# Scores in three PSUM banks, first-pass chunks in two, and GpSimd masking two rows of probabilities at once

## The chip, the core and the metric

The kernel runs on one NeuronCore of a Trainium2 chip, as one program launched once. The metric is the device time in microseconds; three runs are timed, and their median counts. TensorE multiplies into PSUM (eight banks of 128 x 512 float32), VectorE and ScalarE read PSUM, GpSimd works on SBUF alone, and SP issues most of the DMAs.

## The reference

The input is x of shape (8, 1024, 128). Two blocks follow one another, each with a residual sum:

```
x = x + attention(layernorm(x))      # 8 heads of 16, relative positions, softmax over 1024 keys, output projection
x = x + moe(layernorm(x))            # router, best 2 of 8 experts, each (128 -> 2 x 512, gelu gate, 512 -> 128)

xh      = layernorm(inputs)*gamma+beta, split into heads
q, k, v = xh @ Wq + bq, xh @ Wk + bk, xh @ Wv + bv
p       = positions @ Wp
score   = ((q + u) . k + rel_shift((q + v) . p)) / sqrt(128)
ctx     = softmax(score) . v
```

`rel_shift` makes the position score of query q and key k come from position k - q + 1023 for k <= q, zero for k = q + 1, and from the next query's row above that. The kernel handles this with two forms of the operands, one for the lower triangle (QL) and one for the upper (QU), against a common K.

## The kernel before, in words

**Stages.** A prologue normalizes and projects the first batches and runs the first pass of two heads. A hardware loop over the 8 batches follows, with the engines' programs written out for 8 heads of 9 units each (`h`, `u`). Behind it a short tail finishes the last batch and the router's tables, and the expert stage (`expert_phase`) works through the routed tiles. The change touches the first two stages and renames a few banks of the tail.

**Two passes over the scores.** Softmax needs the row maximum first, so each head's scores are computed twice. The first pass (`first_pass`, lines 654 to 676) runs two heads ahead (`AHEAD = 2`): 18 chunks a head, 16 of them of 128 queries by 512 keys and two (positions 8 and 12 of `ORDER`) of four 128x128 diagonal blocks. TensorE writes chunk n to the PSUM bank `pA[n % S1_BUFS]`; VectorE reads it with a masked sum and maximum (lines 1084 and 1090) and counts `s1_read`. TensorE waits for that count before it overwrites the bank: `S1_BUFS` is 3. After a head's chunks VectorE reduces the maxima (`mneg`, 1098) and subtracts them from the super-diagonal score (`dsup`, 1100). The negated maxima go through TensorE, an evacuation and a DMA (`maximum_row`) into one row of the operands.

The second pass (`second_pass`, 678 to 697) has for each head one unit of the 8 upper diagonal blocks (u = 0) and one for each block row of keys (u = 1 to 8), each in two halves of 512 queries. Halves 0 and 1 of every unit use the two halves of `pB` (two banks). ScalarE's exponentials (986, 988) write them to `upper_diag` or to the ring `prob` of four rows. A half is overwritten when its own exponential of the unit before is done (`p_exp`).

**The order on TensorE.** In each unit: score half 0, chunk 2u, score half 1, chunk 2u + 1; then in the units of `PAIRS_AT` = 1, 4, 6, 8 the contexts of two block rows (`context`, line 708, four column strips each); then the small matmuls that `M_AT`, `W_AT`, `PROJECT_AT` and `UPPER_AT` place at this (h, u): maximum rows, turned contexts, output projection, router, and the projections of later batches. Those go to the banks `pM` and `pE`. With pC for the contexts all eight banks are taken: 3 + 2 + 1 + 1 + 1.

**The order on the others.** VectorE: chunk 2u, a small evacuation if `DVE_OUT` has one here, chunk 2u + 1, then other work placed by (h, u): the normalizing of the contexts (1118 to 1128), statistics, the router, and `low` (1069), which subtracts the rounded high half of an operand from the operand (halves of c, k, gl, gu, eight in a batch; gu is read from PSUM). ScalarE: the two exponentials, then evacuations. GpSimd: after a unit's exponentials it masks (`affine_select`) the upper diagonals (564), or, for a block row, sets one element (569), masks its 128x128 diagonal block (571) and adds the upper one (576); then work placed by (h, u): positions (480 to 492), reciprocal roots, residual bias, and the row scatters (518). `context` waits for `p_mask`, the exponential of a later row for `pv_done`. SP loads a head's operands (`stack`), and stores the split operands (`store`) of the next batch in heads 2, 3 and 4, on `hi_done` and `low_done`.

The lines as the profile numbers them:

## Time and profile before

| | us |
|---|---|
| median of three runs | 1681.2 (1679.35 to 1681.27) |
| the profiled execution | 1680.72 |
| its span, first to last instruction | 1679.0 |
| TensorE busy | 1548.0 (92%) |
| VectorE busy | 1397.8 (83%) |
| ScalarE busy | 1108.9 (66%) |
| GpSimd busy | 1103.0 (66%) |
| mean share of the full TensorE clock granted | 0.952 |

An engine's busy time is the union of its instructions' times. TensorE's ends are modelled, since matmuls are pipelined, so a busy TensorE may still be waiting; PEld is its weight loading, which runs beneath the matmul before, and whose start is where a wait ends. The loop lasts from about 87 to 1236 us. Inside it the chain of what ended last can't be read from the page, because the page's chain covers the expert stage; the stretches, waits and timeline below are used for it.

### The profile page before, as it was taken

Reading aid. Unit: us, or ns where it says so; the run is one execution under the profiler, and the core shown is the slowest. Engines: PE = TensorE matmul, PEld = TensorE weight load, DVE = VectorE, ACT = ScalarE, POOL = GpSimd, SP = SyncE. Lnnn points to the kernel's source line nnn. Section 1 sums busy time; section 2 is a strip of 40 time slices with the busy share of each in tenths; the row PEclk is TensorE's granted clock in tenths of the full one; section 3 lists DMA queues with packets and bytes.
Section 4 is the critical chain, followed back from the end, with each engine's and each line's share of the span. In section 5 each row is a group of like instructions: output and inputs, shape, how many; then the busy total and the mean of one; then the engine's idle time right before and its main releaser. Section 6 shows DMA issues by size and latency. Waiting matters only on the chain. (4 is left out here: it accounts for less than half of the span.)

```text
span 1679.0 us, 50905 instructions
## 1 busy us (share of the span) xinstructions
PE 1548.0 (92%) x12492; PEld 1204.6 (72%) x12493; DVE 1397.8 (83%) x5262; ACT 1108.9 (66%) x2295; POOL 1103.0 (66%) x2088
## 2 busy tenths in 40 slices
PE   3789999999999999999999999999952699999997
PEld 1567776677777767777777776776741699999997
DVE  4669899989989987998998899899864588887886
ACT  2157777776777776677777777767730477777775
POOL 5247767767766775777677677667673276666665
PEclk8679999999999998999999999999985799999999
DMA  5746535535644553464365355346454244444443
GB/s 136 198 116 174 148 93 152 164 96 128 180 116 128 161 148 84 110 203 110 104 174 148 93 141 164 97 129 179 122 153 136 42 58 54 56 56 52 56 53 49
DMA packets 133844, 199.72 MB, mean 119 GB/s; under 512 B 20888, under 2 KB 95016, under 8 KB 133632
## 3 DMA queue, kind: packets, MB, share of 16 engines
q1 hardware_dynamic: 108064, 177.07, 39.0%
q0 software_dynamic: 25568, 20.14, 8.2%
q8 instruction: 94, 1.54, 0.4%
q14 instruction: 118, 0.97, 0.2%
HBM read 108.10 MB, written 75.20 MB: 109 GB/s over the span
## 5 line engine op out<-in xcount | busy, mean ns | idle before, releaser
L1084 DVE CUSTOM_DVE_ANT_0 junk<-pA,lmask 128x512 bf16<-128x512 f32 x1056 | 686.9, 683 | 65.1 <-PE pA L671 45.9
L986 ACT ACTIVATE prob<-pB 128x512 f32<-128x512 f32 x384 | 229.8, 598 | 205.5 <-PE pB L690 115.9
L1578 POOL DMA_INDIRECT out<-yb,dst x142 | 230.4, 1622 | 131.3 <-ACT yb L1656 78.5
L692 PE MATMUL pB<-QL,K 97*128 97x512 f32 (+3 forms) x768 | 286.4, 373 | 1.4 <-ACT upper_diag L986 1.2
L669 PE MATMUL pA<-K,QL 96*128 96x512 f32 (+3 forms) x792 | 282.1, 357 | 5.1 <-DMA K<-split_operands 3.4
L690 PE MATMUL pB<-QU,K 97*128 97x512 f32 (+3 forms) x640 | 267.5, 418 | 0.2
L671 PE MATMUL pA<-K,QU 96*128 96x512 f32 (+3 forms) x660 | 233.1, 354 | 4.4 <-DVE acc L1084 3.2
L988 ACT ACTIVATE prob<-pB 128x512 f32<-128x512 f32 x384 | 227.9, 594 | 12.7 <-PE pB L692 3.4
L708 PE MATMUL pC<-prob,vext 128*17 128x256 f32 x3088 | 217.8, 385 | 0.1
L576 POOL TENSOR_TENSOR prob<-prob,upper_diag 128x128 f32<-128x128 f32 x384 | 179.7, 468 | 31.9
L690 PEld LDWEIGHTS pB<-QU,K 97*128 97x128 f32 x640 | 122.0, 191 | 99.9 <-issue 62.3
L518 POOL DMA_INDIRECT routed_rows<-sent,sent_to x144 | 156.9, 1089 | 29.7 <-issue 24.3
L569 POOL MEMSET prob<- 1x1 f32 x384 | 33.9, 88 | 205.6 <-ACT prob L988 197.9
L669 PEld LDWEIGHTS pA<-K,QL 96*128 96x128 f32 x792 | 153.5, 194 | 14.0 <-DVE acc L1084 4.5
L1090 DVE CUSTOM_DVE_ANT_0 junk<-pA,umask 128x128 bf16<-128x128 f32 x528 | 122.2, 284 | 44.1 <-PE pA L675 41.3
L692 PEld LDWEIGHTS pB<-QL,K 97*128 97x128 f32 x768 | 147.3, 192 | 15.7 <-ACT upper_diag L986 2.8
L671 PEld LDWEIGHTS pA<-K,QU 96*128 96x128 f32 x660 | 128.1, 194 | 22.2 <-DVE acc L1084 14.5
L1699 DVE SCALAR_TENSOR_TENSOR g<-pLin,b_all,gl 128x256 f32<-128x256 f32 x288 | 125.8, 478 | 21.4 <-issue 7.9
L708 PEld LDWEIGHTS pC<-prob,vext 128*17 128x17 f32 x3088 | 78.2, 98 | 84.3 <-issue 22.8
L1607 PE MATMUL pY<-w_all,g 128*128 x1136 | 138.4, 275 | 0.0
L1607 PEld LDWEIGHTS pY<-w_all,g 128*128 128x128 f32 x1136 | 133.1, 192 | 0.0
L1649 ACT ACTIVATE gl<-pGate,b_all 128x256 f32<-128x256 f32 x288 | 119.2, 464 | 12.1 <-PE pGate L1601 8.4
(305 smaller groups left out, 3642.9 us busy)
## 6 DMA issues: line engine op xcount, KB each, us to landing
QL<-split_operands SPq DMA_DIRECT2D x67, 256.0 KB
QU<-split_operands SPq DMA_DIRECT2D x67, 256.0 KB
K<-split_operands SPq DMA_DIRECT2D x67, 256.0 KB
xg<-routed_rows SPq DMA_DIRECT2D x75, 132.0 KB
split_operands<-c_h SPq DMA_DIRECT2D x36, 256.0 KB, 6.1
split_operands<-c_l SPq DMA_DIRECT2D x36, 256.0 KB, 6.4
QL<-split_operands SPq DMA_DIRECT2D x67, 128.0 KB
QU<-split_operands SPq DMA_DIRECT2D x67, 128.0 KB
```

The lines of the kernel that those rows point to most:

```text
L518: po.indirect_dma_start(dram["xs"], bass.IndirectOffsetOnAxis(sent_to[:, t, j:j + 1], 0), sent[:, t, :], None).then_inc(scattered, 16)
L576: po.tensor_tensor(p, p, upper_diag[h % 2][:, P * kb:P * kb + P], ALU.add).then_inc(p_mask, 1)
L669: mm = pe.matmul(dst[:, 0:low], QL[0:KROWS, s, q], K[0:KROWS, s, k0:k0 + low], start=True, stop=True)
L671: mm = pe.matmul(dst[:, low:HALF], QU[0:KROWS, s, q], K[0:KROWS, s, k0 + low:k0 + HALF], start=True, stop=True)
L690: mm = pe.matmul(pB[:, q0:q0 + up], K[0:r, s, k], QU[0:r, s, q0:q0 + up], start=True, stop=True)
L692: mm = pe.matmul(pB[:, q0 + up:q0 + HALF], K[0:r, s, k], QL[0:r, s, q0 + up:q0 + HALF], start=True, stop=True)
L708: mm = pe.matmul(pC[VW * strip:VW * strip + D + 1, :], vext[:, kb, h % H, :], prob[kb % RING][:, quarter * strip:quarter * strip + quarter ...
L986: act.activation(p[:, 0:HALF], pB[:, 0:HALF], ACT.Exp, scale=SCALE).then_inc(p_exp, 1)
L988: act.activation(p[:, HALF:S], pB[:, HALF:S], ACT.Exp, scale=SCALE).then_inc(p_exp, 1)
L1084: v.tensor_tensor_reduce(out, src[:, :], lmask[:, at:at + HALF], 1.0, -3.0e38, ALU.add, ALU.max, acc[:, s, qb, n % 2:n % 2 + 1]).then_inc( ...
L1578: po.indirect_dma_start(dram["out"], bass.IndirectOffsetOnAxis(dst[k][:, a:a + 1], 0), yb[k][:, a, :], None, compute_op=ALU.add).then_inc( ...
L1607: mm = pe.matmul(pY[k % 2][:, a, :], g[k % 2][:, c, P * a:P * a + P], keep["w2"][:, bass.ds(ex * F + c * E, E)], start=(c == 0), stop=(c = ...
```

## The change

- PSUM: `S1_BUFS` goes from 3 to 2. `pB` becomes three single banks, and the halves of all units, in order, go round them (`S2_BUFS = 3`, counter g = 2 (9 h + u) + half). A score half waits for the exponential three halves back instead of two.
- TensorE's order: in units with contexts the next unit's score half 0 is issued before the two contexts, not after them and the small matmuls.
- GpSimd masks block rows in pairs, in the even units: two memsets, one select and one addition over both diagonal blocks. For this the ring's rows lie two by two in one tensor (`keep["b2"]` is twice as wide).
- Six of the eight `low` halves of a batch (c, k, gl) and the eight `dsup` differences go from VectorE to GpSimd, the former at `SPLIT_AT`, the latter in unit 3 (`DSUP_AT`). The two halves of gu stay on VectorE and get a semaphore of their own, `gu_low`.
- Places of GpSimd's other work move by a unit or two (positions, residual, scatters). In prologue and tail, `pB[2]` takes the place of the third pA bank.

```diff
-S1_BUFS = 3
+S1_BUFS = 2
+S2_BUFS = 3
...
-        prob = [keep["b2"]] + [sb(f"prob{i}", [P, S]) for i in range(1, RING)]
+        ring = [keep["b2"], sb("prob23", [P, 2, S])]
+        prob = [ring[i // 2][:, i % 2, :] for i in range(RING)]
...
-        pB, pC = pb("pB", [P, S]), pb("pC", [P, S // STRIPS])
+        pB, pC = [pb(f"pB{i}", [P, HALF]) for i in range(S2_BUFS)], pb("pC", [P, S // STRIPS])
...
-        LOW_AT = {(1, 2): 0, (2, 3): 1, (2, 7): 2, (3, 2): 3, (3, 6): 4, (4, 1): 5, (4, 3): 6, (4, 4): 7}
-        POSITIONS_AT = ((1, 1), (1, 4), (1, 8), (2, 1), (2, 4), (2, 6), (5, 4), (5, 6))
+        LOW_AT = {(3, 6): 4, (4, 4): 7}
+        SPLIT_AT = {(0, 3): 0, (1, 8): 1, (2, 8): 2, (3, 3): 3, (3, 7): 5, (4, 2): 6}
+        DSUP_AT = 3
+        POSITIONS_AT = ((1, 1), (1, 3), (1, 7), (2, 1), (2, 3), (2, 5), (5, 5), (5, 7))
...
-        SCATTER_AT = ((0, 1), (0, 4), (0, 6), (0, 8), (1, 6), (3, 1), (3, 6), (3, 8), (4, 4), (4, 6), (5, 1), (5, 8), (6, 1), (6, 4), (6, 6), (6, 8))
+        SCATTER_AT = ((0, 1), (0, 5), (0, 7), (0, 8), (1, 5), (3, 1), (3, 5), (4, 5), (4, 7), (5, 1), (5, 3), (6, 1), (6, 3), (6, 5), (6, 7), (7, 5))
...
+            def low(nb, n):
+                name, half = SPLITS[n]
+                cut = slice(HALF * half, HALF * half + HALF)
+                src = {"c": qu, "k": kc, "gl": g_lo}[name][:, cut]
+                have = known(po, nb * HI_N + n + 1)
+                po.wait_ge(set_pool, POOL_SET)
+                po.wait_ge(hi_done, have)
+                po.tensor_tensor(parts[name][1][:, cut], src, parts[name][0][:, cut].bitcast(F32), ALU.subtract).then_inc(low_done, 1)
+            def super_difference(b, h):
+                ...
+                po.wait_ge(mx_done, have)
+                po.tensor_tensor(dsup[:, s, :], acc[:, s, :, 3], mneg[:, s, :].bitcast(F32), ALU.add).then_inc(dsup_done, 1)
...
-                        else:
-                            kb = u - 1
-                            if kb > 0:
-                                po.memset(prob[kb % RING][0:1, P * kb - 1:P * kb], 0.0)
-                            p = prob[kb % RING][:, P * kb:P * kb + P]
+                        elif u % 2 == 0:
+                            kb = u - 2
+                            both_rows = ring[kb // 2 % 2][:, :, :].rearrange("p a s -> p (a s)")
+                            for k in (kb, kb + 1)[kb == 0:]:
+                                po.memset(prob[k % RING][0:1, P * k - 1:P * k], 0.0)
+                            p = both_rows.rearrange("p (n q) -> p n q", q=P)[:, kb:kb + NB + 2:NB + 1, :]
                             po.affine_select(out=p, in_=p, compare_op=ALU.is_ge, fill=0.0, base=0,
-                                             pattern=[[1, P]], channel_multiplier=-1).then_inc(lower_masked, 1)
+                                             pattern=[[0, 2], [1, P]], channel_multiplier=-1).then_inc(lower_masked, 1)
...
-                            po.tensor_tensor(p, p, upper_diag[h % 2][:, P * kb:P * kb + P], ALU.add).then_inc(p_mask, 1)
+                            po.tensor_tensor(p, p, upper_diag[h % 2][:, P * kb:P * kb + 2 * P].rearrange("p (n q) -> p n q", q=P), ALU.add).then_inc(p_mask, 2)
+                        if u == DSUP_AT:
+                            super_difference(b, h + 1)
+                        if (h, u) in SPLIT_AT:
+                            low(b + 1, SPLIT_AT[h, u])
...
-                pe.wait_ge(p_exp, HPB * (b * (H * S2U) + h * S2U + u) + half + 1)
-                r, q0 = MROW + 1, HALF * half
+                g = HPB * (h * S2U + u) + half
+                pe.wait_ge(p_exp, HPB * (b * (H * S2U)) + max(g, 1))
+                r, q0, dst = MROW + 1, HALF * half, pB[g % S2_BUFS]
...
-                        second_pass(b, h, u, 0)
+                        if (h, u) == (0, 0) or (u - 1) % S2U not in PAIRS_AT:
+                            second_pass(b, h, u, 0)
                         first_pass(b, h + AHEAD, 2 * u)
                         second_pass(b, h, u, 1)
                         first_pass(b, h + AHEAD, 2 * u + 1)
                         if u in PAIRS_AT:
+                            if (h, u) != (H - 1, S2U - 1):
+                                second_pass(b, h + (u + 1) // S2U, (u + 1) % S2U, 0)
                             back, kb = PAIRS_AT[u]
                             context(b, h + back, kb)
                             context(b, h + back, kb + 1)
...
+                                    pe.wait_ge(low_done, (b + 1) * LOW_N + LOW_N)
...
-                v.wait_ge(mx_done, b * H + h + 1)
-                v.tensor_tensor(dsup[:, s, :], acc[:, s, :, 3], mneg[:, s, :].bitcast(F32), ALU.add).then_inc(dsup_done, 1)
...
                 elif name == "super":
+                    v.wait_ge(dsup_done, b * H + H)
                     super_out(src, done)
```

## Rows read from the trace of the kernel before

**Rows 1.** Stretches of the kernel: us, then busy time (instructions) of each engine, clock, DMA share.

```profile
0.00:87.00 87.00, 45.79 (x139) 28.17 (x140) 48.44 (x174) 18.05 (x29) 33.30 (x61) 0.75 0.61 161
...
87.00:1236.00 1149.00, 1133.98 (x9272) 811.29 (x9272) 1033.44 (x4233) 831.39 (x1680) 803.34 (x1848) 0.99 0.49 135
...
1313.00:1679.00 366.00, 352.53 (x3010) 351.94 (x3010) 287.24 (x721) 254.41 (x577) 230.38 (x142) 0.98 0.40 53
```

**Rows 2.** The same view for two batches of the loop.

```profile
237.28:378.78 141.50, 139.93 (x1159) 100.35 (x1159) 129.06 (x529) 103.84 (x211) 100.55 (x231) 1.00 0.50 136
...
520.29:668.07 147.78, 146.29 (x1159) 104.37 (x1159) 129.39 (x529) 104.07 (x211) 100.55 (x231) 0.95 0.47 131
```

**Rows 3.** Waits in 237.28 to 378.78: total us, times, longest.

```profile
PEld pB L696 <- ACT prob L988: 3.0, 7, 0.4
...
PEld pB L690 <- ACT b_all L988: 1.7, 4, 0.4
...
PEld pB L690 <- ACT prob L986: 1.5, 4, 0.5
...
PEld pA L671 <- DVE acc L1084: 1.1, 3, 0.5
...
PEld pM L761 <- DVE hr L1183: 1.3, 1, 1.3
```

**Rows 4.** Groups in that batch, count | busy, mean ns | idle before.

```profile
L708 PE MATMUL pC<-prob,vext 128*17 128x256 f32 x384 | 26.8, 381 | 0.0
...
L708 PE MATMUL pC<-b_all,vext 128*17 128x256 f32 x128 | 10.0, 385 | 0.0
...
L1100 DVE TENSOR_TENSOR dsup<-acc,mneg 128x8 f32<-128x8 f32 x8 | 2.1, 265 | 0.3
...
L1069 DVE TENSOR_TENSOR k_l<-kc,k_h 128x512 fp32r<-128x512 f32 x2 | 1.4, 680 | 0.0
```

**Rows 5.** Timeline, third head of a batch: start, us, engine, line [idle <-releaser].

```profile
708.26 0.67 DVE L1084 CUSTOM_DVE_ANT_0 junk<-pA,lmask 128x512 bf16<-128x512 f32 x1
...
708.83 0.60 ACT L986 ACTIVATE prob<-pB 128x512 f32<-128x512 f32 x1 [0.34 <-PE pB L692]
...
709.00 0.19 PEld L671 LDWEIGHTS pA<-K,QU 96*128 96x128 f32 x1 [0.25 <-DVE acc L1084]
...
709.48 0.19 PEld L690 LDWEIGHTS pB<-QU,K 97*128 97x128 f32 x1 [0.23 <-ACT prob L986]
...
709.77 0.52 PEld L675 LDWEIGHTS pA<-K,QU 96*128 96x128 f32 x4
...
710.07 0.62 ACT L986 ACTIVATE prob<-pB 128x512 f32<-128x512 f32 x1
...
712.01 0.19 PEld L669 LDWEIGHTS pA<-K,QL 96*128 96x128 f32 x1
```

**Rows 6.** Timeline, a load of pA and its read, twice.

```profile
777.52 0.19 PEld L669 LDWEIGHTS pA<-K,QL 96*128 96x128 f32 x1
...
778.25 0.69 DVE L1084 CUSTOM_DVE_ANT_0 junk<-pA,lmask 128x512 bf16<-128x512 f32 x1 [0.33 <-PE pA L671]
...
779.51 0.19 PEld L669 LDWEIGHTS pA<-K,QL 96*128 96x128 f32 x1
...
780.17 0.69 DVE L1084 CUSTOM_DVE_ANT_0 junk<-pA,lmask 128x512 bf16<-128x512 f32 x1 [0.61 <-PE pA L669]
```

**Rows 7.** Timeline, VectorE and GpSimd side by side.

```profile
671.34 1.22 DVE L1118 TENSOR_TENSOR vsh<-vsh,psup 128x1024 f32<-128x1024 f32 x1
...
671.52 1.35 POOL L576 TENSOR_TENSOR b_all<-b_all,upper_diag 128x128 f32<-128x128 f32 x1 [0.17 <-POOL b_all L571]
```

**Rows 8.** GpSimd's groups in 237.28 to 378.78.

```profile
L576 POOL TENSOR_TENSOR prob<-prob,upper_diag 128x128 f32<-128x128 f32 x48 | 22.3, 465 | 4.0
...
L571 POOL TENSOR_SCALAR_AFFINE_SELECT prob<-prob 128x128 f32<-128x128 f32 x48 | 15.0, 312 | 0.0
...
L483 POOL TENSOR_TENSOR g_lo<-rp,cos_lo 128x512 f32<-128x512 f32 x2 | 2.6, 1280 | 0.0
```

More of the change, by code:

```diff
@@ L161, in attention_phase @@
         e_ready, e_done, hi_done = sem("e_ready"), sem("e_done"), sem("hi_done")
-        ln, low_done, pos, norm, rs_done, res_done = (sem(n) for n in ("ln", "low_done", "positions", "norm", "rs_done", "residual_biased"))
+        ln, low_done, gu_low, pos, norm, rs_done, res_done = (sem(n) for n in ("ln", "low_done", "upper_low", "positions", "norm", "rs_done", "residual_biased"))
         placed, moved = sem("head_values_placed"), sem("values_shifted")
@@ L292, in store @@
             def store(nb, name):
-                highs, lows = known(sp, nb * HI_N + READY[name]), known(sp, nb * LOW_N + READY[name])
+                highs, lows = known(sp, nb * HI_N + READY[name]), known(sp, nb * GU_N + GU_N if name == "gu" else nb * LOW_N + LOWS[name])
                 sp.wait_ge(set_dve, DVE_SET)
                 sp.wait_ge(hi_done, highs)
-                sp.wait_ge(low_done, lows)
+                sp.wait_ge(gu_low if name == "gu" else low_done, lows)
                 for op, row in PLACES[name]:
@@ L316, in _ @@
                 sp.wait_ge(hi_done, READY[name])
-                sp.wait_ge(low_done, READY[name])
+                if name == "gu":
+                    sp.wait_ge(gu_low, GU_N)
+                else:
+                    sp.wait_ge(low_done, LOWS[name])
                 store_side(name, 0)
@@ L609, in project @@
                 first = nb == 0 if isinstance(nb, int) else False
-                dst = (pE, *pA)[j % 4] if first else pE
+                dst = (pE, *outside)[j % 4] if first else pE
                 if j == 0:
@@ L695, in second_pass @@
                         k = slice(k0, k0 + P)
-                        mm = pe.matmul(pB[:, k], K[0:r, s, k], QU[0:r, s, k], start=True, stop=True)
+                        mm = pe.matmul(dst[:, k0 - q0:k0 - q0 + P], K[0:r, s, k], QU[0:r, s, k], start=True, stop=True)
                 mm.then_inc(s2_ready, 1)
@@ L788, in small_piece @@
                 elif part == 0 and name == "values 0":
-                    pe.wait_ge(low_done, (b + 1) * LOW_N + LOW_N)
+                    pe.wait_ge(gu_low, (b + 1) * GU_N + GU_N)
                 elif part == 0:
@@ L870, in _ @@
             pe.wait_ge(m_done, m_at(B, "rows 1") + 1)
-            router_hidden(range(NB), pA[1]).then_inc(m_ready, 1)
-            router_fold(B, pA[2]).then_inc(m_ready, 1)
-            router_logits(B, pB[:, 0:HALF]).then_inc(m_ready, 1)
-            router_ranks(B, pB[:, HALF:S]).then_inc(m_ready, 1)
+            router_hidden(range(NB), outside[1]).then_inc(m_ready, 1)
+            router_fold(B, outside[2]).then_inc(m_ready, 1)
+            router_logits(B, pB[0]).then_inc(m_ready, 1)
+            router_ranks(B, pB[1]).then_inc(m_ready, 1)
         @block.scalar
@@ L887, in evacuate @@
                 half = slice(HALF * (j % 2), HALF * (j % 2) + HALF)
-                src = (pE, *pA)[j % 4] if isinstance(nb, int) and nb == 0 else pE
+                src = (pE, *outside)[j % 4] if isinstance(nb, int) and nb == 0 else pE
                 if j < 2:
@@ L1037, in _ @@
                 copied(f"rows {j}", (pE, pA[0])[j], m_done)
-            fold(B, pA[2])
+            fold(B, outside[2])
             tanh(B)
@@ L1068, in low @@
                 v.wait_ge(hi_done, nb * HI_N + n + 1)
-                v.tensor_tensor(parts[name][1][:, cut], src, parts[name][0][:, cut].bitcast(F32), ALU.subtract).then_inc(low_done, 1)
+                v.tensor_tensor(parts[name][1][:, cut], src, parts[name][0][:, cut].bitcast(F32), ALU.subtract).then_inc(gu_low if name == "gu" else low_done, 1)
             def super_out(src, done):
@@ L1299, in _ @@
                 stats(1, t)
-            for n in range(4, LOW_N):
+            for n in range(4, HI_N):
                 low(0, n)
@@ L1370, in _ @@
                 v.wait_ge(w_ready, B * W_N + 1 + j)
-                final(j, pA[1 + j], w_done)
+                final(j, outside[1 + j], w_done)
                 router_stats(B, range(4 * j, 4 * j + 4))
@@ L1375, in _ @@
             v.wait_ge(m_ready, m_at(B, "hidden") + 1)
-            router_bias(B, pA[1])
+            router_bias(B, outside[1])
             hidden_stats(B)
@@ L1386, in _ @@
             v.wait_ge(m_ready, m_at(B, "ranks") + 1)
-            places(B, 0, pB[:, HALF:S])
+            places(B, 0, pB[1])
             for part in (1, 2):
```

37 lines of the change are left out of this document (22 added, 15 removed).

## Prediction

> **What bounds the kernel now.** I read the stretches first: of the 1679.0 us, the loop over the eight batches takes 87 to 1236 us, with TensorE busy for 1134 of 1149, VectorE 1033, ScalarE 831, GpSimd 803; the expert stage after it (366 us, TensorE 352.5 busy) is not touched [rows 1]. So the time is eight times one batch, and a batch at full clock is 141.5 us; one with the clock at 0.95 is 147.8 with the same instructions [rows 2]. Two engines are near that length, TensorE (139.9 busy) and VectorE (129.1). Matmul ends are modelled, so I work out TensorE's own time from starts. Four pieces of 128 columns follow one another by 0.11 (the group at 709.77, of which the last load is 0.19: 0.52). From there to the load at 712.01 are 2.24 us with no other piece: the four (0.44), three runs of 512 columns at 2.4 GHz with their switch, 0.23 each, and so 1.11 for a pair of contexts [rows 5]. A head has 16 score halves and 16 chunks of 0.23, two of each in four pieces (0.45), and four pairs of contexts: 4.58 + 4.58 + 4.44 = 13.6, or 108.6 a batch. The remaining matmuls are 1159 less 384 + 128 of contexts, and by the loops 240 of scores and 240 of the first pass: 167 [rows 2, 4]; at the 0.11 of a 128-column piece, and less for the ranks', 17.5. Own time 126.1, waits 15.4.
>
> Who ends the waits, in the table of waits of one batch: ScalarE's exps 3.0 + 1.7 + 1.5 = 6.2, VectorE's reads of pA 1.1, a VectorE result (the router's hidden rows) 1.3 [rows 3]. The other 6.8 lie under modelled ends; shared out alike, scores cost 11.1, first-pass banks 2.0, results 2.3.
>
> **The score side (removed).** Before, each half of pB is written again only after its exp: the exp of 708.83 ends at 709.43, the load follows at 709.48 and its exp starts at 710.07 [rows 5]: 0.05 + 0.59 + 0.60 = 1.24 a unit, while TensorE alone needs 0.92. With three banks a half waits for the exp three halves back: three per 1.24 is more than TensorE can issue, so the waits on exps go: -11.1 a batch. Issuing the next unit's first half ahead of the contexts adds no matmul; its maximum row was sent four units earlier. ScalarE gets work beneath the contexts except where pv_done still holds it (units 5 and 7: one context, 0.5). ScalarE's 103.8 [rows 2] does not bind.
>
> **The first pass (added).** Chunk k now waits for VectorE's read of k-2. The cycle: the read at 708.26 takes 0.67, and the load waiting for it starts at 709.00, 0.07 after its end [rows 5]; a load at 779.51 has its read start at 780.17 into an idle VectorE, 0.66, and in two pieces, 777.52 to 778.25, 0.73 [rows 6]. Cycle 0.69 + 0.07 + 0.66 = 1.42 per two chunks, against 0.92 of TensorE and 1.22 (2 x 0.61) of VectorE back to back. Three banks made that 1.42 for three chunks, which never bound. I write out a head from loads of chunks, all else absent. Units 0 and 1: chunk 2 waits to 1.48 (TensorE is there at 1.14), chunk 3 to 2.10 (1.94), chunk 4 at 3.67. Units 2 and 3: chunk 6 to 1.48 (0.92), 7 to 2.09 (1.94), 8 to 2.90 (2.55). Units 5 and 7: 0.56 each and 0.15 in the latter. The waits are 0.34, 0.16, 0.56, 0.15, 0.35, 0.56, 0.56 and 0.15: 2.83 a head, 22.6 a batch. But nearly all of the 167 small matmuls stand in units without contexts, after the second chunk and before the waiting one. Set place by place against the waits (for each head and unit the lesser of both) they fill 13.0: 1.7 in unit 0, 2.0 in 2, 2.0 in 3, 4.1 in 5, 3.2 in 7. Left: 9.6. Bounds: 2.0 (the waits of before, if PE work covers the rest) and 22.6.
>
> **VectorE's other work.** Six low halves go to GpSimd (0.68 each) and eight differences of 0.27 [rows 4]: 4.1 + 2.1 = 6.2. The two upper halves stay. So VectorE falls to 122.9. Its chunks are 8 x (16 x 0.61 + 2 x 0.86) = 91.8, leaving 31 of other work. With two banks VectorE is empty during each pair of contexts: from my head, 0.96 after unit 1, 0.68 after 4, 0.66 after 6, 1.23 after 8, 28.2 a batch. The pieces placed there by the code fit but for 2.6 (such as 1.22 in one lump [rows 7]); about 7.8 stand in units without contexts, where they lengthen the cycle directly; formerly a third chunk in store hid them. I take 0.7 of 2.6 and half of 7.8, since the small matmuls stand at the same places: 5.7; bounds 0 and 10.4.
>
> Sum of a batch after: 126.1 + 9.6 + 2.3 + 5.7 = 143.7, 2.2 more than now, 17.6 for eight.
>
> **GpSimd.** A pair of rows now takes two memsets (0.09, overlapping), a select of 256 columns and an addition of 256. The select of 128 is 0.31, so of 256 between that and 0.62; I take 0.42, as its fixed part is large. From 128 and 512 columns (0.465 and 1.280) the addition is 0.74 [rows 8]; with their hand-over 1.3, against 2 x 0.87 before. 32 pairs save some 12 a batch; six low halves of 1.28 and eight differences of 0.2 add 9.3. It stays near 98 of 143. The first row of a pair is ready a unit later than before, but contexts of a pair come two units after its exps: the mask is done about 2.9 us into unit 2 and wanted at 4.0. I cost it at nothing; without that cover it is 0.3 to 0.5 a pair. Low halves arrive before the stores that take them (heads 2, 3, 4), and the last, which gates head 5's reload, is the unmoved upper one. Waits added: super_out on dsup_done (met three units earlier; DVE chunks are behind it), project 0 on low_done (met two heads earlier), the mask's own (as before). SP's queue keeps its order.
>
> **Ends.** The 36 first-pass chunks ahead of the loop have only VectorE at 0.61 and a TensorE at 0.75 of its clock in that stretch [rows 1]. The cycle there is at least 1.42 against 1.22 for half the chunks, but projects between them hide some: +2 (0 to 6). In the tail other banks are named; the waits it moves are met.
>
> Total 1680.7 (the profiled run; 1.7 outside its span) + 17.6 + 2 = 1700. The three timed runs have the median 1681.2, within 0.5 of it.
>
> **GpSimd's port.** A masking addition of 128x128 took 1.35 us at 671.52, beneath a VectorE product of 1.22 that reads two SBUF tensors, against 0.465 as a rule [rows 7, 8]. The Trainium skill, GPSIMD Engine Reference, section Specifications, says that GpSimd shares its SBUF interfaces with VectorE where the latter has two SBUF inputs; the trace agrees. By that rule the pair's mask is held as one, contexts and then TensorE wait, and the sum would be rival 4's, where without it the masks cost nothing.
>
> **Rivals.**
> 1. The score side decides, faster. The first-pass cycle fills wholly with small matmuls and VectorE's lumps fall in its holes: waits on pA fall to about 4, lumps to 1. 126.1 + 4 + 2.3 + 1 = 133.4 is the end; halfway between that and 143.7 is 138.5, or -24, with the +2 of the start 1659. For it: VectorE loses 6.2 us, and the waits on exps that the table names are six times those on pA [rows 3]. Against it: the cycle 1.42 is longer than 1.24. It holds if waits on pA plus lumps stay under 13.1 a batch.
> 2. The two first-pass banks bind, much slower. The mechanism is the 1.42 cycle in units without contexts with only half of the 13.0 filled: 143.7 + 6.5 = 150.2, +70 and +2: 1752. Against it: small matmuls are there in the trace. It is slower from 13.1 on.
> 3. Both cancel, no change: within 0.2% (3.4 us, what a measurement of this kernel can tell from none): 1681. The engines trade one cycle for the other.
> 4. Masks in pairs come late: about seven stretches of VectorE in a batch read two SBUF tensors for as long as that 1.22 (the sums over vsh, the router's normalizing); each holds an addition by 1.35 - 0.465 = 0.9, and if half of that reaches TensorE it is 3.2 a batch on top of 143.7, so 1726. Against it: the pair's mask has a unit to spare, as worked out above.
>
> **Chances.** Forecast 0.40 (its own range 1685 to 1720, from 7 to 12 left over of the first-pass waits and 4 to 8 of lumps), rival 1 0.34, rival 2 0.12, rival 3 0.10, rival 4 0.04. Part of the forecast's lower edge meets rival 3. Faster 0.35, same 0.10, slower 0.55. The range reaches from 1648 (two thirds of rival 1) to 1738 (the lower half of rival 2); a dip of the clock as in the fourth batch, 6.3 us [rows 2], is within it either way.
>
> **What would show it.** Right: TensorE's waits on ScalarE near zero; loads of pA waiting for VectorE in most units 2, 3, 5, 7, first-pass loads 1.4 apart from the chunk two before; VectorE busy 123 a batch with longer idle stretches after contexts; a batch of 143 to 145. The masking addition 0.74, select 0.42, low halves 1.28 on GpSimd. Wrong: a batch under 141, pA loads hardly waiting (then the small matmuls fill more than place by place), or contexts waiting for GpSimd's addition.

## The result, and the profile after

The changed kernel takes 1732.6 us (median of four runs, 1728.2 to 1736.2), the kernel before 1681.2 (four runs, 1679.4 to 1690.4): a ratio of 1.0293, 95% interval 1.0249 to 1.0337. It is slower by 51, where 19 were forecast (17.6 in the batches and 2 at the start). The profiled execution's span is 1730.9 against 1679.0.

The stretches of the kernel after, in the view of [rows 1]: start, loop, expert stage.

```profile
0.00:97.00 97.00, 53.70 (x144) 32.66 (x146) 49.01 (x172) 18.06 (x29) 33.54 (x62) 0.67 0.56 147
97.00:1288.00 1191.00, 1161.69 (x9253) 817.69 (x9252) 1009.37 (x4121) 835.00 (x1679) 771.85 (x1448) 0.98 0.47 130
1365.00:1731.00 366.00, 352.00 (x3010) 351.42 (x3010) 287.34 (x721) 254.36 (x577) 232.55 (x143) 0.98 0.40 53
```

Two batches of it, one with a dip of the clock (to be laid beside [rows 2]):

```profile
400.10:552.55 152.45, 149.12 (x1159) 105.08 (x1159) 126.44 (x515) 104.42 (x211) 96.55 (x182) 0.96 0.46 126
698.95:845.26 146.31, 143.01 (x1159) 101.10 (x1159) 126.11 (x515) 104.30 (x211) 96.57 (x182) 1.00 0.48 132
```

A batch at full clock went from 141.5 to 146.3 with the same 1159 matmuls. The 52 us fall into: the start, whose first exp of the loop moved from 88.2 to 97.1 (+8.8); eight batches of +4.85 (+38.8); the clock, which beyond the loop's first 13 us stood at its lower level for 31 us of the loop after and for 17 before, a little under half of which is lost, and what else the first batch differs by (+5); and the rest (-0.6). The expert stage is the same.

Where the time went, in the table of waits of the second of these batches (total, times, longest), against [rows 3]:

```profile
PEld pA L702 <- DVE acc L1123: 10.4, 25, 1.1
...
PEld pC L742 <- issue: 6.6, 25, 0.4
...
PEld pA L702 <- issue: 5.9, 13, 0.7
...
PEld pA L704 <- DVE acc L1123: 3.9, 11, 0.6
...
PEld pM L796 <- DVE hr L1220: 1.1, 1, 1.1
```

All waits on ScalarE are gone from it, and VectorE's reads took their place: 14.3 us listed in two rows where 1.1 stood in one. But a part of either list is no wait of that kind. The first load behind each of the 32 pairs of contexts in a batch finds TensorE's loading idle for 0.42 us, before and after, whoever is named as its releaser. Before, that is 18 loads of pB named "issue" (7.6 us, no releaser), 12 named an exp (5.1) and 2 of pM; after, 18 named a read of VectorE (7.6). Without these, waits on exps were 1.9 us in 5 places before, and waits on VectorE's reads went from 1.4 to 8.0.

The masks' groups in the same batch, against [rows 8]:

```profile
L605 POOL TENSOR_TENSOR prob<-prob,upper_diag 128x256 f32<-128x256 f32 x17 | 14.1, 831 | 2.5
L605 POOL TENSOR_TENSOR b_all<-b_all,upper_diag 128x256 f32<-128x256 f32 x16 | 12.2, 760 | 2.4 <-POOL b_all L600 0.2
...
L600 POOL TENSOR_SCALAR_AFFINE_SELECT prob<-prob 128x256 f32<-128x256 f32 x16 | 6.5, 404 | 0.0
...
L511 POOL TENSOR_TENSOR c_l<-qu,c_h 128x512 fp32r<-128x512 f32 x2 | 2.6, 1281 | 0.0
...
L519 POOL TENSOR_TENSOR dsup<-acc,mneg 128x8 f32<-128x8 f32 x8 | 1.6, 206 | 2.2 <-ACT prob L1027 2.1
```

Select 0.40, addition 0.76 to 0.83, low half 1.28, difference 0.21, where the prediction had 0.42, 0.74, 1.28 and 0.2.

The start, in the timeline after at the lower clock: reads of chunks come in twos.

```profile
77.10 0.69 DVE L1123 CUSTOM_DVE_ANT_0 junk<-pA,lmask 128x512 bf16<-128x512 f32 x1
77.24 0.29 PEld L702 LDWEIGHTS pA<-K,QL 96*128 96x128 f32 x1 [0.97 <-DVE acc L1123]
...
78.18 0.69 DVE L1123 CUSTOM_DVE_ANT_0 junk<-pA,lmask 128x512 bf16<-128x512 f32 x1 [0.39 <-PE pA L704]
...
78.80 0.69 DVE L1123 CUSTOM_DVE_ANT_0 junk<-pA,lmask 128x512 bf16<-128x512 f32 x1
```

The load at 77.24 had its bank back 0.14 into the read that started at 77.10, and its own read starts at 78.18, 0.94 later (0.73 at full clock for such a chunk in two pieces [rows 6]). So two chunks take 78.80 - 77.10 = 1.70 at the lower clock, not 1.42; before, with three banks, reads came 0.61 apart at the lower clock too, 1.22 for two.

### The profile page after: what moved, and what is told of

It is laid out like the page before. It is cut to its first block and busy times, and to the rows that moved or that the text cites. A ratio compares the mean times of both kernels' runs of the same rounds, so it can differ in the third digit from the quotient of the medians.

```text
span 1730.9 us, 50465 instructions
## 1 busy us (share of the span) xinstructions
PE 1583.4 (91%) x12492; PEld 1214.9 (70%) x12493; DVE 1374.3 (79%) x5148; ACT 1112.8 (64%) x2295; POOL 1074.6 (62%) x1689
## 5 line engine op out<-in xcount | busy, mean ns | idle before, releaser
L1123 DVE CUSTOM_DVE_ANT_0 junk<-pA,lmask 128x512 bf16<-128x512 f32 x1056 | 696.7, 686 | 113.3 <-PE pA L704 81.9
L702 PE MATMUL pA<-K,QL 96*128 96x512 f32 (+3 forms) x792 | 321.4, 407 | 25.9 <-DVE acc L1123 13.4
L724 PE MATMUL pB<-QU,K 97*128 97x512 f32 (+3 forms) x640 | 246.0, 384 | 0.0
L704 PE MATMUL pA<-K,QU 96*128 96x512 f32 (+3 forms) x660 | 242.3, 369 | 3.4 <-DVE acc L1123 2.4
L1025 ACT ACTIVATE prob<-pB 128x512 f32<-128x512 f32 x256 | 153.2, 598 | 94.8 <-PE pB L726 41.6
L1025 ACT ACTIVATE b_all<-pB 128x512 f32<-128x512 f32 x256 | 152.5, 596 | 86.0 <-PE pB L724 46.2
L1027 ACT ACTIVATE b_all<-pB 128x512 f32<-128x512 f32 x256 | 152.8, 597 | 80.4 <-PE pB L726 71.7
L1027 ACT ACTIVATE prob<-pB 128x512 f32<-128x512 f32 x256 | 152.6, 596 | 45.8 <-PE pB L726 37.7
L742 PE MATMUL pC<-b_all,vext 128*17 128x256 f32 x2048 | 139.5, 391 | 0.0
L742 PE MATMUL pC<-prob,vext 128*17 128x256 f32 x2064 | 138.2, 386 | 0.8 <-POOL prob L605 0.8
```

The source lines that it names most:

```text
L702: mm = pe.matmul(dst[:, 0:low], QL[0:KROWS, s, q], K[0:KROWS, s, k0:k0 + low], start=True, stop=True)
L704: mm = pe.matmul(dst[:, low:HALF], QU[0:KROWS, s, q], K[0:KROWS, s, k0 + low:k0 + HALF], start=True, stop=True)
L724: mm = pe.matmul(dst[:, 0:up], K[0:r, s, k], QU[0:r, s, q0:q0 + up], start=True, stop=True)
L742: mm = pe.matmul(pC[VW * strip:VW * strip + D + 1, :], vext[:, kb, h % H, :], prob[kb % RING][:, quarter * strip:quarter * strip + quarter ...
L1025: act.activation(p[:, 0:HALF], pB[HPB * n % S2_BUFS][:, :], ACT.Exp, scale=SCALE).then_inc(p_exp, 1)
L1027: act.activation(p[:, HALF:S], pB[(HPB * n + 1) % S2_BUFS][:, :], ACT.Exp, scale=SCALE).then_inc(p_exp, 1)
```

## The experiments

All batches below are at full clock, first exp to first exp. Ratios are by the timed runs, with the 95% interval, to the kernel before as it was timed again beside each group of runs (1682.6 to 1684.9, so only the changed kernel's ratio is over 1681.2). In e10 part of the probabilities keeps old values, so its results aren't the layer's.

| run | banks: chunks, scores | batch | loop begins | median | ratio |
|---|---|---|---|---|---|
| before | 3, 2 | 141.5 | 88.2 | 1681.2 | |
| after | 2, 3 | 146.3 | 97.1 | 1732.6 | 1.0293 (1.0249 to 1.0337) |
| e1 banks only | 2, 3 | 146.2 | 98.1 | 1732.5 | 1.0281 (1.0255 to 1.0307) |
| e2 moves only | 3, 2 | 143.1 | 89.3 | 1694.5 | 1.0059 (1.0042 to 1.0075) |
| e3 two and two | 2, 2 | 146.3 | 96.4 | 1725.1 | 1.0249 (1.0204 to 1.0293) |
| e4 start on three | 2, 3 | 146.3 | 88.8 | 1720.4 | 1.0217 (1.0188 to 1.0245) |
| e5 five in common | 5 | 141.8 | 91.1 | 1685.2 | 1.0011 (0.9986 to 1.0037) |
| e6 the same, with the moves | 5 | 142.0 | 91.1 | 1691.7 | 1.0048 (1.0025 to 1.0071) |
| e7 after, order of before | 2, 3 | 146.6 | 97.3 | 1727.1 | 1.0253 (1.0193 to 1.0312) |
| e8 after, half reads | 2, 3 | 139.7 | 94.1 | 1668.6 | 0.9912 (0.9876 to 0.9949) |
| e9 before, half reads | 3, 2 | 138.7 | 84.3 | 1659.9 | 0.9845 (0.9793 to 0.9898) |
| e10 neither bound | 5 | 137.6 | 84.7 | 1657.5 | 0.9831 (0.9788 to 0.9874) |
| e12 pairs only | 3, 2 | 142.4 | 91.4 | 1693.4 | 1.0048 (1.0018 to 1.0077) |
| e13 before, half chunks | 3, 2 | 128.9 | 85.4 | 1592.2 | 0.9444 (0.9390 to 0.9498) |
| e14 after, half chunks | 2, 3 | 129.4 | 90.2 | 1591.2 | 0.9438 (0.9360 to 0.9515) |
| e15 low halves and places | 3, 2 | 142.7 | 91.0 | 1696.8 | 1.0067 (1.0040 to 1.0094) |

The medians hold their share of the clock's dips (e1 and e3 have the same batch and differ by 7 in the median), so conclusions are drawn from batches.

**Which part costs.** e1 has the change's edits of banks and order alone, e2 the other edits alone, e3 takes the bank from the chunks and gives it to nobody in the loop (`S1_BUFS = 2`, `S2_BUFS = 2`, the order of before).

```diff
 e1 on before:                            e2 on after:
-S1_BUFS = 3                             -S1_BUFS = 2
+S1_BUFS = 2                             -S2_BUFS = 3
+S2_BUFS = 3                             +S1_BUFS = 3
+(first half ahead of the contexts)      +S2_BUFS = 2
                                         -(first half ahead of the contexts)
```

> The kernel before with the bank change alone (two first-pass banks, three score banks, the next unit's first half ahead of the contexts); VectorE keeps its low halves, differences and the places of its small work, GpSimd masks row by row. Theory A, the two first-pass banks bring the whole loss of the loop (4.85 us a batch, 146.35 against 141.5), and VectorE's 6.2 us a batch of moved work only softened it: a batch of 147.5 to 149.5, 1742 to 1758. Rival B, the banks are neutral and the loss comes from what went to GpSimd and from the new places of the small work: a batch near 142, 1690 to 1700 with the slower start.

> The changed kernel with three first-pass banks and two for the scores again, and the order of the matmuls of before; pairs of rows, low halves and differences on GpSimd stay. Theory A: the loss is gone, and since VectorE was not what the chain of before waited for in most units, its 6.2 us a batch bring little: a batch of 140 to 141.5, 1668 to 1682. Rival B: masks in pairs and low halves from GpSimd are late: a batch of 144 to 146, 1700 to 1718.

> The kernel before with two first-pass banks and two score banks (one bank for nothing but the start's projections), same order, nothing moved: what the lost bank costs by itself. Theory A: TensorE's waits on VectorE come on top of those on ScalarE, which stay, with some of both in the same places: a batch of 150 to 157, 1760 to 1815. Rival C, the third score bank (and the half issued ahead of the contexts) does the harm and not the lost one: a batch of 142 to 144, 1690 to 1705.

One full-clock batch of e1, e2 and e3 in turn (length; TensorE, its loads, VectorE, ScalarE and GpSimd busy):

```profile
995.26:1141.46 146.20, 143.33 (x1159) 100.77 (x1159) 130.17 (x529) 104.28 (x211) 101.89 (x231) 1.00 0.47 132
```

```profile
527.99:671.08 143.09, 140.24 (x1159) 100.26 (x1159) 125.30 (x515) 103.84 (x211) 96.26 (x182) 1.00 0.49 135
```

```profile
696.38:842.68 146.30, 143.85 (x1159) 100.70 (x1159) 130.07 (x529) 104.67 (x212) 101.99 (x231) 1.00 0.46 132
```

The lost bank is the whole loss of the batches, theory A, but less than I expected of e1 and e3. e3 and e1 have the same batch to 0.1 us: the third score bank, together with the half issued ahead of the contexts, is worth nothing in sum. Their heads are not the same. The second takes 16.7 us in e1 and 17.9 in e3, the third 18.6 and 18.1, the eighth 18.7 and 18.1, from first exp to first exp. The changed kernel against e7 below, which differ in the order alone, shows the same pattern (16.2 and 17.4, 17.9 and 17.4, 18.6 and 18.0), so it is the order that moves time from head to head.

e1 and the changed kernel have the same batch too, though VectorE is busy for 130.2 in one and 126.1 in the other: with two banks its moved work is worth nothing in sum either. There too gains and losses cancel: the second and third heads are 0.6 and 0.7 shorter in the changed kernel, the first, fourth, fifth and sixth 0.3, 0.6, 0.4 and 0.3 longer. With three banks the moves cost 1.6, and e2's 143.1 lies between both theories.

**The start.** In e4 the 36 chunks ahead of the loop go round pA0, pA1 and the third score bank, each waiting for the read three chunks back.

```diff
-                dst = pA[n % S1_BUFS]
+                ahead = isinstance(b, int) and h < AHEAD
+                dst = outside[(S1U * h + n + 2) % 3] if ahead else pA[n % S1_BUFS]
```

> The changed kernel, but the 36 chunks ahead of the loop go round three banks (the third score bank is free there). The chunks' reads came 0.62 and 1.08 apart there, 1.70 for two, where they were 1.22 before, over some 18 pairs: 8.6 us, and the loop began at 97.1 instead of 88.2. Theory A': the start is the cycle over two banks at half clock, so it comes back whole: the loop begins at 88 to 89, 1724. Rival: the start lost its stretch of full clock for another reason, and the cycle is only 3.6 of it: the loop begins at 93 to 94, 1729.

Reads of that start, in e4's timeline, go from bank to bank 0.61 apart (here at full clock, in the kernel before at the lower one as well):

```profile
73.63 0.69 DVE L1129 CUSTOM_DVE_ANT_0 junk<-pA,lmask 128x512 bf16<-128x512 f32 x1
...
74.25 0.69 DVE L1129 CUSTOM_DVE_ANT_0 junk<-pB,lmask 128x512 bf16<-128x512 f32 x1
...
74.86 0.69 DVE L1129 CUSTOM_DVE_ANT_0 junk<-pA,lmask 128x512 bf16<-128x512 f32 x1
```

The loop begins at 88.8, as theory A' has it, but the two banks are not the whole of the start's loss. In this stretch the executions also differ in how long TensorE had its full clock: 10 us in the kernel before, none in the changed one, 7 us in e4. From the first read to the first exp of the loop, in before, e12, after, e3 and e4 in turn:

```profile
58.40:88.24 29.84, 24.04 (x85) 15.06 (x83) 24.68 (x102) 4.09 (x7) 2.49 (x2) 0.67 0.71 192
```

```profile
58.26:91.35 33.09, 28.96 (x85) 18.62 (x83) 24.68 (x102) 4.09 (x6) 2.49 (x2) 0.50 0.63 174
```

```profile
57.35:97.07 39.72, 30.89 (x85) 18.80 (x84) 25.25 (x100) 4.08 (x7) 2.69 (x3) 0.50 0.54 146
```

```profile
58.38:96.38 38.00, 28.91 (x85) 17.27 (x84) 25.85 (x102) 4.09 (x7) 2.49 (x2) 0.59 0.53 147
```

```profile
57.50:88.78 31.28, 26.52 (x85) 16.72 (x83) 24.31 (x100) 4.09 (x6) 2.70 (x3) 0.61 0.67 184
```

At the lower clock throughout, two banks take 39.7 (after) and three 33.1 (e12; 32.7 in e15); with 7 us at full clock 38.0 (e3) and 31.3 (e4). So the banks cost 6.6 to 7.0. The remainder of the 8.8 is the full clock that the kernel before had (33.1 - 29.8 = 3.3), less 1.1 by which the first read came earlier in the changed kernel. The missing stretch doesn't go with the banks: e12 and e15 have three and none of it, e3 and e11 have two and 7 and 14 us of it.

**Order, and banks in common.** e7 puts the score half behind the contexts again; in e5 and e6 halves and chunks, in the order in which TensorE issues them, take the next of five banks, and each waits for the reader of that bank.

```diff
 e5 and e6:
-                dst = pA[n % S1_BUFS]
+                dst = pA[bank_of(f)]
...
-                r, q0, dst = MROW + 1, HALF * half, pB[g % S2_BUFS]
+                wait_user(b, 2 * g)
+                r, q0, dst = MROW + 1, HALF * half, pA[TURN[2 * g]]
```

> The changed kernel with each score half issued where it was before, behind the contexts. Theory A: the first-pass cycle sets the batch, the half's place is worth nothing: 146.2 to 146.8 a batch, 1728 to 1738. Rival: the half ahead of the contexts holds TensorE there for its exp or gives ScalarE work, so the batch moves by over 1 us either way.

> The kernel before, but score halves and first-pass chunks, which TensorE issues in turn, take the next of five banks in common; order and everything else as before. A chunk's bank is then wanted again by the score half three further on, a half's bank by the chunk two further on: each has 2.5 of its own kind to spare, where it is 3 and 2 before. Theory A (each side has a cycle of 1.42 and 1.24 us and stops TensorE when it gets under two of a kind; at two banks the first pass alone sets the batch, 146.3 with either two or three score banks): at 2.5 both cycles are shorter than the engines' own rates, 0.57 and 0.50 us against 0.61 and 0.60, so the batch falls below 141.5, to 134 to 139: 1625 to 1665. Rival: with any bank less than three for the chunks VectorE's other work in one lump reaches TensorE, and each kind now also waits for the other engine: 143 to 146, 1695 to 1720.

> The same five common banks with the pairs of rows, low halves and differences on GpSimd. Those moves cost 1.6 us a batch with the banks of before (143.1 against 141.5) and nothing with two (146.35 against 146.25). Theory A: with five in common VectorE is nearest to the bound, and its 6.2 us less a batch are worth 1 to 3: 132 to 137. Rival D, GpSimd's later results cost wherever the banks do not: 1 to 2 a batch more than with five banks alone.

A batch of e7, e5 and e6 in turn:

```profile
549.48:696.11 146.63, 143.35 (x1159) 100.89 (x1159) 126.25 (x515) 104.92 (x210) 96.43 (x182) 1.00 0.48 131
```

```profile
239.53:381.37 141.84, 139.62 (x1159) 100.58 (x1159) 129.45 (x529) 104.19 (x212) 100.14 (x231) 1.00 0.49 136
```

```profile
239.66:381.66 142.00, 138.58 (x1159) 100.19 (x1159) 125.13 (x515) 103.83 (x210) 96.05 (x182) 1.00 0.49 136
```

The order is worth 0.3. e5 was a miss for both theories: 2.5 banks for each side ought to have freed both, and the batch is that of before. So was e6: with five banks the moves cost 0.2, neither a gain nor 1 to 2. That raised the question of whether there was anything to free.

**What is under the waits.** e8 and e9 shorten VectorE's read of the chunks off the diagonal, e10 shortens reads and most exps on five common banks, e13 and e14 shorten reads and matmuls of those chunks.

```diff
 e8, e9, e10, e13, e14:
-                    v.tensor_tensor_reduce(out, src[:, :], lmask[:, at:at + HALF], 1.0, ...
+                    v.tensor_tensor_reduce(out[:, 0:HALF // 2], src[:, 0:HALF // 2], lmask[:, at:at + HALF // 2], 1.0, ...
...
 e13, e14 besides:
+                    wide, low = HALF // 2, min(low, HALF // 2)
...
-                    if low < HALF:
-                        mm = pe.matmul(dst[:, low:HALF], ...
+                    if low < wide:
+                        mm = pe.matmul(dst[:, low:wide], ...
```

> The changed kernel, but each chunk that isn't on the diagonal is read over its first 256 columns only (the maximum then covers half of the keys; it only keeps the exps small). A read then takes some 0.4 us instead of 0.67 and the cycle some 1.15 instead of 1.42; VectorE has 128 x 0.27 = 34 us a batch less. Theory A: the two banks' cycle is what the batch waits for, so most of the waits on VectorE go (33.7 us gross of lost load time before first-pass loads): 130 to 136 a batch, 1615 to 1655. Rival: the waits are TensorE's own small matmuls and contexts, wrongly read: over 142.

> The kernel before (three first-pass banks, two score banks) with chunks off the diagonal read over 256 columns only, as in the same edit of the changed kernel, which went from 146.35 to 139.7 us a batch. Theory F (the floor is near: TensorE's own work is 137 or more a batch, not 126.1, so no cycle of banks has more than a few us to give): 138.5 to 140.5 a batch, 1650 to 1665. My prediction's numbers (own work 126.1, 11.1 of waits on the exps, 2.0 on pA): the waits on the exps stay, only 2 go: 139.5 to 141. Rival V (VectorE's 129 us of work is what sets the batch of before, TensorE has 15 to spare): under 136.

> Five banks in common, chunks off the diagonal read over 256 columns, and six of the nine rows of probabilities of a head computed over half of their columns only (the other half keeps old values, so later results are not the layer's): both cycles are gone, what is left is TensorE's own work and its waits on small results. Theory F: 136 to 139 a batch, that is, my own time of 126.1 was 8 to 11 too small and the waits of before only some 4. My prediction's own time: 126.1 + 2.3 of results: 128 to 131 a batch.

> The kernel before with chunks off the diagonal computed and read over 256 columns only (the maximum covers half of the keys). Against the same with 512 computed and 256 read (138.7 a batch) it only takes TensorE work: 14 chunks a head less 0.11 and 2 less 0.05, 13.1 us a batch. Theory F (TensorE's own work is what the batch of before is made of): most of it comes off, less what the exps' cycle of 1.24 us a unit then holds in units without contexts (0.92 - 0.22 = 0.70 of TensorE there): 128 to 134 a batch, 1580 to 1625. Rival G (another chain, GpSimd's masks or a DMA, holds the batch near 138 whatever TensorE has to do): 136.5 to 138.7.

> The same edit of the changed kernel (139.7 with half the reads alone). Theory F: TensorE's 13.1 come off here too, less what two first-pass banks hold (the cycle with short reads, some 1.15 for two chunks, against 0.70 of TensorE), while three score banks let go of the exps' cycle: 129 to 136, near the other. If it ends under that of before by over 1 us, three score banks are worth something once TensorE is out of the way. Rival G: 137.5 to 139.7.

A batch of e8, e9, e10, e13 and e14 in turn:

```profile
939.15:1078.81 139.66, 138.17 (x1159) 100.95 (x1159) 96.72 (x515) 103.25 (x211) 95.48 (x182) 1.00 0.50 138
```

```profile
519.24:657.92 138.68, 138.39 (x1159) 100.33 (x1159) 100.17 (x529) 103.93 (x212) 101.76 (x231) 1.00 0.51 139
```

```profile
657.63:795.21 137.58, 136.84 (x1159) 100.47 (x1159) 101.42 (x529) 87.25 (x211) 101.03 (x231) 1.00 0.50 140
```

```profile
628.90:757.82 128.92, 127.64 (x1128) 91.21 (x1126) 98.94 (x529) 103.78 (x212) 100.45 (x231) 1.00 0.53 150
```

```profile
614.87:744.25 129.38, 125.77 (x1128) 91.80 (x1127) 95.46 (x515) 102.24 (x212) 95.24 (x182) 1.00 0.53 149
```

The groups of reads and exps in that batch of e10:

```profile
L1114 DVE CUSTOM_DVE_ANT_0 junk<-pA,lmask 128x256 bf16<-128x256 f32 x128 | 53.3, 421 | 23.1 <-PE pA L689 13.5 <-PE pA L687 6.8
```

```profile
L1017 ACT ACTIVATE prob<-pA 128x256 f32<-128x256 f32 x48 | 18.5, 385 | 5.5 <-PE pA L721 4.8
L1015 ACT ACTIVATE prob<-pA 128x256 f32<-128x256 f32 x48 | 18.4, 384 | 30.3 <-PE pA L719 18.0 <-PE pA L721 12.3
```

With VectorE's reads (0.42 instead of 0.68) and most exps (0.38 instead of 0.60) shortened, the batch is 137.6, and TensorE's busy column, 136.8, agrees with it. The batch of before, 141.5, gave up 3.9 in all: 2.8 to the shorter reads (e9), 1.1 to the shorter exps (e10, which also changes the banks). In this batch of e10 no load waits for a read or an exp, save the 32 idle times of 0.42 us behind contexts, so some 4 us is also the most that any arrangement of banks could have given. The batch after gave up 6.6 to the reads (e8), a miss for both theories there (under 136, over 142).

Most of the 137.6 is TensorE's own work, and not another chain, by e13: taking 13.1 us of its columns away and nothing else shortens the batch from 138.7 to 128.9, by 9.8, with the same work on GpSimd and ScalarE. Loads of scores that don't stand behind contexts then wait for exps for 6.2 us, against 2.0 in e9, which may be where the other 3.3 went. Even there, where TensorE has time for ScalarE, three score banks and two first-pass banks (e14) end 0.5 behind.

**Small matmuls.** e11 and e16 issue every matmul of the loop's projections twice.

```diff
-                    mm = pe.matmul(dst[:, lo:hi], w[:, :], src[:, at + lo:at + hi], start=True, stop=True)
+                    for _ in range(1 if first else 2):
+                        mm = pe.matmul(dst[:, lo:hi], w[:, :], src[:, at + lo:at + hi], start=True, stop=True)
```

> The changed kernel with each matmul of the projections in the loop issued twice (24 of 256 columns and 8 transposes of 128 a batch): the same results, and the small work that I let fill TensorE's waits is larger by 24 x 0.22 + 8 x 0.11 = 6.2 us (the loads behind one of 256 columns are 0.22 apart, so these were undersized by half in my sum too). My prediction's rule (small matmuls fill the waits place by place): under 2 of it shows, 146.4 to 148.3. Theory F: most waits stand elsewhere and little is filled: 4.5 to 6.2 show, 150.9 to 152.5.

> The kernel before with each matmul of the projections in the loop issued twice, as in the same edit of the changed kernel: its batches, clear of dips of the clock, went up by 8 or more there, 4.8 of it in the eighth head with a stop of up to 4.2 us ahead of the next head's first scores, 1.25 in the third. Own work added: 6.2. Theory F: it is on the path here as well, 5 to 6.2 and no less in the third head than with two banks (1.25), 146.5 to 148 or more where the stop appears too. My prediction's rule (waits take it up): under 2.

Both whole times (1805.3 and 1771.7) are of little use, and both lie above what either rule had without the stop that follows. In either kernel TensorE stopped for 3.6 to 5.0 us at the end of every batch, at the load of the diagonal scores that begin the next one, and the clock dipped in every batch. The third and fourth heads are clear of both. The third has eight of the doubled matmuls, the fourth none. From first read to first read, the third head and then the fourth, in the kernel before and in e16:

```profile
415.13:431.37 16.24, 16.24 (x134) 11.39 (x133) 15.87 (x71) 11.82 (x25) 12.23 (x27) 1.00 0.67 185
431.37:449.62 18.25, 17.76 (x144) 12.35 (x142) 16.93 (x63) 13.76 (x28) 13.83 (x35) 1.00 0.67 197
```

```profile
448.81:466.67 17.86, 17.86 (x142) 12.89 (x140) 16.09 (x70) 11.79 (x25) 13.07 (x27) 1.00 0.66 185
466.67:484.60 17.93, 17.49 (x144) 12.39 (x142) 16.63 (x62) 13.76 (x28) 13.40 (x35) 1.00 0.63 186
```

Eight more matmuls of 256 columns lengthen the third head by 1.62 us, 0.20 each, none of it hidden there, but the fourth head is 0.32 shorter: 1.3 of the 1.6 is left. In e11 the third head rose by 1.25 (17.38 to 18.63), and 0.4 of that came back in the next: 0.9 of 1.6. So with three first-pass banks a fifth of the added work is taken up by waits, with two a little under half. What causes the stop was not looked into.

**The moves.** e12 is the kernel before with the pairs of rows alone, e15 with the other moves alone.

```diff
 e12 on before (e15 has the rest of the change's edits outside the banks):
-                            kb = u - 1
+                        elif u % 2 == 0:
+                            kb = u - 2
...
+                            po.tensor_tensor(p, p, upper_diag[h % 2][:, P * kb:P * kb + 2 * P]...).then_inc(p_mask, 2)
```

> The kernel before with only GpSimd's masking changed to two rows at a time; banks, low halves, differences and places as before. All moves together cost 1.6 us a batch with these banks (143.1). If the pairs bring it (the first row of a pair is masked a unit later): 142.5 to 143.2 a batch. If the low halves, differences and new places of small work do: 141.4 to 141.7.

> The kernel before with low halves, differences and the new places of the small work, but masks row by row, banks of before. All moves cost 1.6 us a batch, the pairs alone 0.9 (142.4 against 141.5). If they add up: 142.1 to 142.3 a batch, 1686 to 1692. Rival: VectorE's 6.2 us less are worth something once the pairs don't hide it: 140.0 to 141.4.

A batch of each:

```profile
532.67:675.06 142.39, 140.19 (x1159) 100.34 (x1159) 129.56 (x530) 103.92 (x211) 89.31 (x168) 1.00 0.50 135
```

```profile
814.21:956.87 142.66, 140.13 (x1159) 100.25 (x1159) 125.22 (x515) 103.84 (x211) 107.54 (x245) 1.00 0.48 135
```

Each by itself costs about 1 (142.4 and 142.7, both just outside what was expected), together 1.6. In e15 it lies in the fourth and fifth heads (19.2 against 18.2, 18.5 against 18.2); by which wait was not settled. What the runs show is that less of VectorE's work brought nothing in sum in any arrangement (e2, e15, e6 against e5, the changed kernel against e1). The work itself was less than I took it for: VectorE's busy time fell by 3.8 to 4.3 us in these pairs of runs, not by 6.2.

## Why the prediction was wrong

The side was right and so was the culprit, the first-pass banks. The size failed: +4.85 a batch where the sum had +2.2, and of the 32 us that the forecast fell short, 21 are this, 7 the start and 5 the clock. The forecast's own range (to 1720) missed the time; the whole range held it only because it reached up into rival 2, and that is no merit of the sum. By the steps:

- **"Own time 126.1, waits 15.4": wrong, and the root of the rest.** This is the step that failed first. e10 gives 137.6 for own time and results together, where I had 126.1 + 2.3 = 128.4. Two errors can be named. A pair of contexts was priced at 1.11 from the one group of [rows 5]; over the 102 pairs of the loop of before between 700 and 1150 us, from the load ahead of a pair to the load behind it, the mean is 1.46, less that chunk's own 0.23: 1.23, or +3.9 a batch. The one group itself gives no less (rows below): from the chunk's load at 710.32 to the load at 712.01 are 1.69, less two runs 1.23. I had taken off three runs of 512 columns, but the third is that of the load at 711.90, and the load at 712.01 follows it by 0.11, so its columns can hardly lie between. The 32 small matmuls of 256 columns (projections and upper form) were priced as pieces of 128, 0.11; e16 measures 0.20: +2.9. That leaves some 2.4 not accounted for. I had set the busy column aside as modelled: 139.9 of 141.5 in [rows 2] was nearer the truth than my sum.

```profile
710.32 0.19 PEld L669 LDWEIGHTS pA<-K,QL 96*128 96x128 f32 x1
...
710.91 0.13 PEld L708 LDWEIGHTS pC<-b_all,vext 128*17 128x17 f32 x8 [0.40 <-POOL prob L576]
...
711.90 0.19 PEld L690 LDWEIGHTS pB<-QU,K 97*128 97x128 f32 x1 [0.42 <-issue]
...
712.01 0.19 PEld L669 LDWEIGHTS pA<-K,QL 96*128 96x128 f32 x1
```

- **"Shared out alike, scores cost 11.1".** I took the 6.2 of listed waits on exps [rows 3] and scaled them to fill the false 15.4. Measured, they are worth 0 with two first-pass banks (e3 against e1, with the order) and 1.1 with VectorE's reads short (e10 against e9). The traces show why. Of the 17 loads that are listed as waiting for exps, 12 stand behind a pair of contexts, where all 32 loads of a batch find the same 0.42 us idle; that time belongs to the pair, and faster exps can't take it away. It stays in e10, at 32 loads again, 28 of them put down to VectorE. The other 5 loads are 1.9 us, near the 1.1 measured. What the 0.42 us are is open: the loads run beneath the matmuls ahead of them, so TensorE may still be streaming.
- **"Left: 9.6" and "I take ... 5.7".** Against 2.0 before, these were +13.3 for the lost bank; measured, the exps' side being worth nothing, it is +4.8. Both the gain of 11.1 and this loss of 13.3 were too large, and what they left, +2.2, came out too small: the lost bank was not paid for by a gained one. The two terms of the loss can't be told apart further. That the moved work of VectorE changes nothing in sum with two banks (e1 against after) speaks against lumps as a cost, though single heads did move by up to 0.7. And the moved work was mis-sized: 6.2 by durations, 4.0 by the busy time.
- **"They fill 13.0": probably too much.** Three quarters of the small work (13.0 of 17.5) was to vanish in waits. Of added small matmuls of the same kind a little under half did, in the third and fourth heads with two first-pass banks (e11). How far those already there fill the waits, no run here measures.
- **"Ends ... +2 (0 to 6)": wrong by 6.8.** The start lost 8.8, of which 6.6 to 7.0 are the two banks and the rest mostly the clock of the single execution. The cycle was priced at full clock though [rows 1] showed 0.75 for that stretch: at the lower level (1.2 GHz) it is 1.70 a pair against 1.22. Over 18 pairs that would be 8.6; what was measured is less, so not every pair paid it in full.
- **GpSimd at nothing:** its operations took about what was forecast, and with two banks the moves are free in sum; with three they cost 1.6, which the prediction did not have. Its list of waits passed over one on GpSimd that was there before: loads of contexts waited 1.9 us in 6 places for the masking addition. In e12 that row is down to 0.4 and the batch is 0.9 longer, so the row doesn't tell the cost. GpSimd's port (rival 4) shows no sign in the batch: e1, with single masks, has the changed kernel's.
- **Rivals and signs.** Rival 1 rested on the same 11.1 and falls with it: the score side was not what held the kernel. Rival 2's mechanism is what happened, in part: 146.3 lies between the forecast's 143.7 and its 150.2. Of the signs, the waits on ScalarE went, as forecast; the batch (143 to 145) and VectorE's busy time (123, measured 126.1) were off.

The clock's dips took 5 us more than in the execution before; e7, with two dips of 3.4 us beyond the loop's first 20 us, and e8, with none beyond its first 10, have two first-pass banks as well, so the dips don't come with those.

## What to carry to other kernels

Before waits are priced, find the floor by shortening the suspected cycles (shorter reads, shorter exps) or by adding a known amount of work: a sum of own work from a few best samples makes it too small, and all that it lacks turns up as waits that a change then seems to remove. If the engine's busy column says 99% and the sum says 89%, doubt the sum. And a wait listed at a load is not a saving. See first whether loads at the same place in the program idle for the same time whoever is named (here 0.42 us behind every pair of contexts), then take the wait out alone (here the waits on exps, by two and by three score banks beside the same two first-pass banks) and see whether the batch moves. Where two runs have the same batch, compare them head by head before calling a part worth nothing: gains and losses may cancel. And before a difference in a short stretch is put down to the change, look at the clock that each execution had there.

## What was not expected of the hardware

A read of a chunk over 256 columns takes 0.42 us on VectorE against 0.68 over 512, and an exp 0.38 against 0.60 on ScalarE: by the difference, a fixed part of 0.16 to 0.17 in each. From a load to the start of the read of its product in two pieces went 0.73 us at full clock [rows 6] and 0.94 at the lower one.

e13 and e14 are 5.6% faster than the kernel before, and e9 1.5%. They take the maximum, which only keeps the exps small, over the first 256 of every 512 keys and over the diagonals. That gives the reference's outputs on its inputs, but guards the exps less: a score that is far above all others in the part left out could overflow them. Where that can be lived with, TensorE's columns are what to take away, not its banks.
